# Transposes of probabilities three heads behind the scores instead of two, weighting of values in halves

## The reference, cut to what matters

```
x = x + attention(group_norm(x))
x = x + deformable(group_norm(x))

attention: windows of 16 x 16 tokens (N = 256), 8 heads of 16 channels
  q, k, v = split(xw @ qkv_w.T + qkv_b)
  attn = softmax(q @ k.T * 16 ** -0.5 + bias[head])     # 256 x 256 per head and window
  out  = attn @ v, then the projection
```

## Time and profile before

| | us |
|---|---|
| median of 3 runs | 3354.45 (3354.16 to 3354.75) |
| the profiled execution, its own time | 3350.4 |
| its span, first to last instruction | 3348.7 |
| mean granted TensorE clock | 0.963 of full speed |

### The profile page before, as it was taken

One profiled execution on the slowest core, in us unless ns is written; L12 is line 12 of the kernel. 1 busy time (PEld: TensorE's weight loads), 2 busy tenths in 40 slices (PEclk: granted clock), 3 DMA queues, 4 the chain that ended last, 5 costly groups with the idle time before them and its releaser, 6 DMA issues.

```text
span 3348.7 us, 78453 instructions
## 1 busy us (share of the span) xinstructions
PE 2717.4 (81%) x22424; PEld 2178.8 (65%) x22424; DVE 2716.9 (81%) x6553; ACT 1882.3 (56%) x3529; POOL 1102.7 (33%) x1525
## 2 busy tenths in 40 slices
PE   0599999999999999995665999897856699989886
PEld 0355655565556655563555888887845598888885
DVE  5488888888888888885656999998945599999996
ACT  0488888888888888885262444442204544434420
POOL 0333333333333333332415322135421241115550
PEclk9999999999999999998898999998978899999998
DMA  6788888888888888885642333233365333333334
GB/s 221 126 142 140 146 136 142 139 144 137 143 139 147 136 142 138 141 143 109 199 138 84 99 97 98 93 99 88 89 242 160 110 118 94 96 96 98 105 91 161
DMA packets 350617, 432.47 MB, mean 129 GB/s; under 512 B 42224, under 2 KB 275072, under 8 KB 344304
## 3 DMA queue, kind: packets, MB, share of 16 engines
q1 hardware_dynamic: 338544, 423.85, 56.5%
q0 software_dynamic: 11904, 6.44, 1.6%
HBM read 283.33 MB, written 147.09 MB: 129 GB/s over the span
## 4 chain that ended last, share of the span: by engine, by line
DVE 19%; DMA 8%; issue 8%; PE 6%; POOL 6%; POOLq 2%; DVEq 1%; ACT 1%; SPq 1%; ACTq 0%
DVE prod L1536 11%; DVE tt L1520 2%; PE sum_ps L1297 2%; DMA vring<-vals 2%; DMA vals<-vring 2%; DMA vring<-attended 2%; DVE x L1547 2%; POOL gath L1113 2%; POOLq L1120 1%; PE wt_ps L1275 1%; DMA o_sel<-off_out,pos 1%; DVE my L1515 1%; PE sum_ps L1237 1%; POOL i_sel L1113 1%; PE om_ps L1260 1%
## 5 line engine op out<-in xcount | busy, mean ns | idle before, releaser
L587 ACT ACTIVATE prob<-sbias,nmax 128x256 f32<-128x256 f32 x2048 | 905.0, 501 | 196.1 <-DVE nmax L674 194.1
L1536 DVE TENSOR_TENSOR prod<-vring,wt_ps 128x1920 f32<-128x1920 f32 (+3 forms) x512 | 902.7, 1816 | 58.9 <-DMA vring<-vals 49.2
L674 DVE CUSTOM_DVE_ANT_0 sbias<-s_ps,nbias 128x256 f32<-128x256 f32 x2048 | 766.9, 421 | 224.3 <-PE s_ps L479 211.8
L1297 PE MATMUL sum_ps<-d_ident,prod 128*128 128x128 f32 x6400 | 758.7, 276 | 23.5 <-DVE prod L1536 23.5
L492 PE MATMUL pt_ps<-a_ident,prob 128*128 128x128 f32 x4096 | 644.3, 280 | 134.1 <-ACT prob L587 131.6
L1297 PEld LDWEIGHTS sum_ps<-d_ident,prod 128*128 128x128 f32 x6400 | 721.4, 143 | 38.4 <-DVE prod L1536 31.6
L492 PEld LDWEIGHTS pt_ps<-a_ident,prob 128*128 128x128 f32 x4096 | 447.3, 140 | 277.6 <-DVE probT L683 118.4
L479 PE MATMUL s_ps<-stack 96*128 96x256 bf16 x2048 | 396.2, 274 | 9.5 <-DMA stack<-parts_dram 9.5
L683 DVE COPY probT<-pt_ps 128x512 f32<-128x512 f32 x512 | 351.7, 687 | 11.8 <-PE pt_ps L492 11.7
L423 POOL CAST parts<-qk 128x1024 bf16<-128x1024 f32 x64 | 66.3, 1036 | 860.1 <-ACT qk L580 860.1
L1403 ACT COPY ssum<-sum_ps 128x512 f32<-128x512 f32 x64 | 37.5, 586 | 513.6 <-PE sum_ps L1307 513.6
(11 more groups left out here) (166 smaller groups left out, 3489.9 us busy)
## 6 DMA issues: line engine op xcount, KB each, us to landing
stack<-parts_dram SPq DMA_DIRECT2D x768, 128.0 KB, 7.4
vring<-vals SPq DMA_DIRECT2D x270, 320.0 KB
parts_dram<-parts SPq DMA_DIRECT2D x64, 768.0 KB, 6.5
off_out<-off SPq DMA_DIRECT2D x64, 432.0 KB
strips<-x SPq DMA_DIRECT2D x68, 256.0 KB, 3.6
a_stats_in<-x SPq DMA_DIRECT2D x16, 1024.0 KB, 4.9
far_sums<-nothing SPq DMA_DIRECT2D x64, 256.0 KB, 2.1
attended<-on SPq DMA_DIRECT2D x256, 64.0 KB
```

The source lines that it names most:

```text
L587: ins = nc.scalar.activation(prob[:, n % 4, half, :], sbias[:, n % SBIAS, half, :], ACT.Exp, bias=nmax[:, n % SBIAS, half:half + 1], scale ...
L674: ins = nc.vector.tensor_tensor_reduce(out=sbias[:, n % SBIAS, half, :], in0=s_ps[:, n % 2, half, :], in1=nbias[:, h, half, :], scale=1.0, ...
L1297: mm = nc.tensor.matmul(sum_ps[:, par, r * H:(r + 1) * H], prod[:, r % 2, dx, dy * C:(dy + 1) * C], ident[:], start=(r + dx + dy == 0), st ...
L1536: nc.vector.tensor_tensor(prod[:, r % 2, first:last].rearrange("p a (t c) -> p (a t) c", c=CG), vring[:, at:at + wide].rearrange("p a (t c ...
```

## The change

The lag of the transposes goes from 2 to 3 slots (T_LAG), and with it the lags of the two copies out (READ_LAG_A from 3 to 4, READ_LAG_V from 2 to 3), so that both copies now fall in even slots. The weighting of four heads is given in two halves of four matmuls: the first in slots 0, 4, 8, 12, the second in slots 1, 5, 9, 13; the waits stand before the first half, the signal behind the second. The steps behind it move with it: `read_o` to slots 5 and 13, `turn_out` to slots 7 and 15, and the two `norm` to slot 8 and, since slot 15 + 1 belongs to the next pair, slot 0 of the next pair. In the text below "the norm of window 0" is the latter. SP's order of issues is not touched. At the end of the stage DVE norms both windows of the last pair, and PE weighs two groups of heads instead of one.

```diff
--- before.py
+++ after.py
@@ -30,11 +30,12 @@
 VA = 32
 SBIAS = 8
 SCALE = float(HD) ** -0.5
-T_LAG = 2
-READ_LAG_A, READ_LAG_V = 3, 2
-PV_LAG = 4
+T_LAG = 3
+READ_LAG_A, READ_LAG_V = 4, 3
+PV_AT, PV_REST = 4, 5
+PV_LAG = 5
+OUT_AT = 7
 Q_AT, K_AT, V_AT = 0, 4, 8
-OUT_AT = 6
 AHEAD = 2
 GN_EPS = 1e-5
 CHUNK = 4 * W
@@ -493,21 +494,22 @@
                                                  prob[:, n % 4, half, kh * P:(kh + 1) * P], ident[:])
                 mm.then_inc(t_done, 1)
 
-            def weigh(p, k, par):
+            def weigh(p, k, par, kh):
 
                 w, t = divmod(k, 2)
-                pe.wait_ge(t_read_a, count(NH * p + 2 * k + 2))
-                pe.wait_ge(t_read_v, count(NH * p + 2 * k + 2))
-                if k == 0:
-                    pe.wait_ge(v_read, count(p + 1))
-                if t == 0:
-                    pe.wait_ge(o_read, count(2 * p + w))
-                for kh in range(2):
-                    for j in range(4):
-                        mm = nc.tensor.matmul(o_ps[32 * j:32 * j + VA, t * NT:(t + 1) * NT],
-                                              va[:, par, 2 * w + kh, 4 * t + j, :],
-                                              probT[:, (4 * k + j) % 8, kh, :], start=(kh == 0), stop=(kh == 1))
-                mm.then_inc(pv_done, 1)
+                if kh == 0:
+                    pe.wait_ge(t_read_a, count(NH * p + 2 * k + 2))
+                    pe.wait_ge(t_read_v, count(NH * p + 2 * k + 2))
+                    if k == 0:
+                        pe.wait_ge(v_read, count(p + 1))
+                    if t == 0:
+                        pe.wait_ge(o_read, count(2 * p + w))
+                for j in range(4):
+                    mm = nc.tensor.matmul(o_ps[32 * j:32 * j + VA, t * NT:(t + 1) * NT],
+                                          va[:, par, 2 * w + kh, 4 * t + j, :],
+                                          probT[:, (4 * k + j) % 8, kh, :], start=(kh == 0), stop=(kh == 1))
+                if kh == 1:
+                    mm.then_inc(pv_done, 1)
 
             def turn_out(win, w):
 
@@ -527,11 +529,13 @@
                         turn(p, n - T_LAG)
                     elif not first:
                         turn(p - 1, n - T_LAG + SLOTS)
-                    if n % 4 == 3:
-                        if n > 3:
-                            weigh(p, (n - 7) // 4, par)
-                        elif not first:
-                            weigh(p - 1, 3, 1 - par)
+                    for kh, at in enumerate((PV_AT, PV_REST)):
+                        if n % 4 == at % 4:
+                            k = (n - 4 - at) // 4
+                            if k >= 0:
+                                weigh(p, k, par, kh)
+                            elif not first:
+                                weigh(p - 1, k + 4, 1 - par, kh)
                     if n == OUT_AT and not first:
                         turn_out(2 * p - 1, 1)
                     if n == NH + OUT_AT:
@@ -557,7 +561,9 @@
             pair(PAIRS - 1, 1, left=0)
             for n in range(SLOTS - T_LAG, SLOTS):
                 turn(PAIRS - 1, n)
-            weigh(PAIRS - 1, 3, 1)
+            for k in (2, 3):
+                for kh in range(2):
+                    weigh(PAIRS - 1, k, 1, kh)
             turn_out(2 * PAIRS - 1, 1)
 
         @block.scalar
@@ -704,8 +710,8 @@
                         read_turned(p if m >= 0 else p - 1, m % SLOTS)
                     if n == OUT_AT + 1 and not first:
                         norm(2 * p - 1, 1, 1 - par, (p - 1) // 2)
-                    if n == NH + OUT_AT + 1:
-                        norm(2 * p, 0, par, p // 2)
+                    if n == (NH + OUT_AT + 1) % SLOTS and not first:
+                        norm(2 * p - 2, 0, 1 - par, (p - 1) // 2)
                     if n == V_AT + 1 and left >= 1:
                         read_v(p + 1, 1 - par)
 
@@ -720,7 +726,8 @@
             for m in range(SLOTS - READ_LAG_V, SLOTS):
                 if m % 2 == 1:
                     read_turned(PAIRS - 1, m)
-            norm(2 * PAIRS - 1, 1, 1, (PAIRS - 1) // 2)
+            for w in range(2):
+                norm(2 * PAIRS - 2 + w, w, 1, (PAIRS - 1) // 2)
 
 
 def deformable(nc, x, attended, w_proj, bproj_row, w_value, bv_row, w_om, bom_row, w_out, b_out, vals, off_out, info_out, far_sums, out):
```

## The result

The changed kernel takes **3396.6 us** (median of 4 runs, 3395.26 to 3411.2) against 3354.4 us before: a ratio of **1.0136**, 95% interval 1.012 to 1.0152, 42 us slower. The forecast was 3386 us, range 3366 to 3407. The profiled execution has a span of 3393.7 us, 45.0 more than before, and all of that arises in the first stage: the second stage's first loads (`vring<-attended`) are issued at 1627.08 us instead of 1581.16, 45.9 later.

A forecast was written before the change was run, and what follows sets the result against it. Compute waits pace pairs at 22.35 us, `stack` landing hidden just under; the change closes a loop of 0.05 + 2.65 + 0.46 + 19.7 = 22.9 us, 62 x 0.52 = 32 us more: 3354.45 + 32 = 3386 us, range 3366 to 3407.

The forecast's parts named there:

- the second one: Hidden bound in the attention stage: `stack` must land before a pair's first scores, with a mean slack of 1.3 us.
- The loop's length: Chain once per pair, stack landed, first scores, maximum, copy, norm, stores, restack, stack landed: 22.9 us.
- landing to first scores: From the landing of `stack` to the pair's first scores on PE: 0 to 0.2 us, taken as 0.05.
- first scores to stores: First scores through maximum, copy and norm on DVE to the issue of window 0's stores: 3.1 us instead of 1.40.
- stores to last landing: From the issue of window 0's stores on SP to the landing of the last `stack` transfer: mean 19.7 us.
- The compute side: Pair's compute period with transposes one slot later: 21.4 us, between 20.3 and 22.35, about half of PE's `exp` wait gained.
- The halves "at nothing": Weighting in halves on PE: 1 entry more per group of four, costed at nothing within the 21.4 us a pair.
- The first rival: The loop does not bind and compute sets the pace: 0.95 us a pair less, 3294 us; chance 0.07.
- The rule on bandwidth: 1 MB read in 6.15 us at 341 GB/s; twelve 128 KB restack loads would take under 5 us.
- The signs: Expected in the profile after: spacing 22.7 to 23.1 us, PE waiting for `stack` about 1.4 a pair, `exp` wait almost gone.

The follow-up runs named there:

- e1: Changed kernel with SP issuing the stores of window 0 of the pair before behind the next restack instead of ahead of it: 3329.63 us, ratio 0.9921.
- e4: Changed kernel with the norm of window 0 at the head of slot 0 on DVE, ahead of `bias_max` of head 0: 3335.28 us, ratio 0.9936.
- e10: Changed kernel with the whole weighting in slots 1, 5, 9 and 13, SP's order kept: 3389.73 us, ratio 1.0102.
- e9: e1 with the whole weighting in slots 1, 5, 9 and 13 instead of halves: 3273.34 us, ratio 0.9755.
- e6: e1 with the whole weighting in slots 0, 4, 8 and 12 instead of halves: 3435.62 us, ratio 1.0251.
- e8: Changed kernel with the norm of window 0 in slot 0 ahead of the copy of head 13 instead of behind it: 3356.55 us, ratio 1.0008.
- e3: Kernel before with only the norm of window 0 moved from slot 15 to slot 0 of the next pair: 3366.3 us, ratio 1.0034.
- e7: Changed kernel with SP's clearing store and load of strips behind the restack instead of ahead of it: 3368.93 us, ratio 1.0045.

## Why the prediction was right

**Which bound decides.** Right: the second one, the landing of `stack`, which no wait of the profile before named. Its slack of 1.3 us was the number that mattered. e1, e4 and e10 show it from three sides, and so does the distance from landing to first scores, 0.12 us in 59 of 61 pairs.

**The loop's length.** Forecast 22.9 us, measured 23.16. The terms, from the chain above and the means of the trace: landing to first scores 0.12 (I took 0.05, inside its bounds); first scores to stores 3.26 instead of 3.11; stores to last landing 3.86 + 15.88 = 19.74 instead of 19.7. The second is the one mis-sized. I took 0.28 us from the reciprocal to the products, from the row at 810.72, where the row of window 0 itself, at 799.94, carries an idle time of 0.19 "<-DVE rsum". Its reciprocal stands at

```profile
799.51 0.25 DVE L689 RECIPROCAL rsum<-x_ps 128x16 f32<-128x16 f32 x1
```

so that there, as after the change (823.37 to 823.80), it is 0.43. A step of a chain should be read from the row whose surroundings are the chain's. The transfers were 0.04 longer, and in two pairs something else than the stack came last, 0.03. Together that is 0.29 us, 17 us over the 60 pairs. Of these 2 come back at the start and 1.5 behind the pairs, and 3 because the median of the runs stood 4.0 us above the profiled execution before and only 1.3 after. So the time came out 11 us above the forecast, in its range.

**The compute side.** Forecast 21.4 us a pair inside 20.3 to 22.35, measured 22.00 (e1). The bound above held, the middle was too hopeful. The halves "at nothing" are the step that the runs speak against: the whole weighting, one slot behind the projections, makes a pair 0.96 us shorter (e9 against e1). A half takes 0.64 us in the changed kernel (the row at 822.25) and the whole 1.07 (e6), some 0.8 us a pair more, and with the halves the waits for ACT's copy stand where the waits for `exp` were. How the 0.96 divides between the two was not measured. It did not touch the time, since the loop covered it, as the prediction had said it would.

**Norm and copy.** The prediction had the copy in its sum as 0.61 us. Taken out of the change (e8), it brings the stores 0.60 us forward, the pair 0.78 and the time 40. That the norm's move without the copy would cost little was in the prediction's numbers, 22.9 - 0.6 = 22.3 us, no more than the pair had before; I did not see it until e3, which measured 11 us.

**The first rival** (the loop does not bind, 3294 us) fell, with its price: even with the loop open the lag and halves give 3330. **The rule on bandwidth** that the prediction took from the Trainium skill (DMA: Bandwidth & Descriptors, section Bandwidth: 1 MB at 341 GB/s, measured for loads to 128 partitions) does not hold for these loads: by it twelve of 128 KB would move in under 5 us, an estimate, and they took 15.4 to 15.9 us from the first issue to the last landing, with the DMA engines full in between the earlier trace rows.

**The signs.** PE's wait for `stack` was forecast at 1.4 us a pair and is 46.1 / 49.7 = 0.93, since compute had less to spare; the spacing was to be 22.7 to 23.1 and is 23.16; stores to landing was to be within 19 to 20.5 us and is 19.74; the wait for `exp` is gone and the second stage unchanged, as forecast.

**Left open:** the lag of 3 was not timed without the halves and the moves of `turn_out` and the norms, so its own share of the compute gain is not known.

## What to carry to other kernels

Before a step is moved to another slot, look up what is queued behind whoever waits for it: here the norm's stores stood ahead of twelve loads in the one queue of SP, the next pair's first scores waited for these loads, and the moved norm waited for the first scores. A transfer that lands 1.3 us before its use leaves no wait in the profile (nor did one that landed 0.27 us before), so compare landing times with first uses where the DMA engines are busy. When a bound is suspected, ease the other side: an edit that is worth 0.96 us a pair with the loop open and 0.13 with it closed names the bound better than any sum.

## What the runs showed of the hardware

The twelve rearranged loads of a restack took 15.4 to 15.9 us on average from the first issue to the last landing in all kernels, whatever ran beside them and wherever in the pair they stood. A plain 256 KB load queued behind them landed 8.5 to 10.1 us after its issue, for 3.1 to 4.9 ahead of them, and POOL waited up to 6.7 us for it (e7): in SP's queue it had to wait for what was in front of it. And eight matmuls in one piece, in a slot with another block or in the next one, differ by 2.6 us a pair (e6 and e9). With four such pieces a pair this is 0.65 us each, beside their own 1.07 us. In e6 PE itself waits for ACT's copy 44.5 us over the stretch, 0.9 us a pair, and e9's view has no such wait. For the rest a likely reason, not tried by itself, is that two buffers of scores are all that DVE has while PE is in such a block.
